# Gated recurrence and feed-forward kernel: y of blocks 0 and 1 from high and low parts, block 0 gated inside the second sweep, another order up to the second iteration

## The reference

```python
u = x @ W_in + b_in                       # 256 -> 64
g = sigmoid(x @ W_gate + b_gate)          # 256 -> 256
for t in range(4096):                     # the recurrence
    h = tanh(h @ A + u[t] @ Bm)
    y[t] = g[t] * (h @ C.T + u[t] @ D.T) + (1 - g[t]) * x[t]
x1 = layernorm(x + (y @ W_out + b_out + x))
hid = gelu(x1 @ bw1.T + b1)               # bw = mean|w| * sign(w), exact gelu
out = layernorm(x1 + (hid @ bw2.T + b2))
```

## Time and profile before

| | before |
|---|---|
| median of three | 446.37 us |
| profiled execution, its own time | 446.38 us |
| its span | 444.6 us |
| PE busy | 424.6 us, 96% |
| DVE busy | 361.0 us, 81% |
| ACT busy | 309.9 us, 70% |
| POOL busy | 302.3 us, 68% |

### The profile page before, as it was taken

How to read it: one execution, slowest core, us unless ns; L and a number is a source line. 1 busy time by engine, 2 the same in 40 slices (tenths; PEclk the granted TensorE clock), 3 DMA queues, 4 the chain that set the end, 5 groups by cost and what they waited for, 6 DMA issues and landing times.

```text
span 444.6 us, 8039 instructions
## 1 busy us (share of the span) xinstructions
PE 424.6 (96%) x2687; PEld 303.4 (68%) x2687; DVE 361.0 (81%) x791; ACT 309.9 (70%) x570; POOL 302.3 (68%) x302
## 2 busy tenths in 40 slices
PE   7999999999998899999999999999999999999882
PEld 4788887777554576776867767677676776766651
DVE  3666687744772889999999999999999999998584
ACT  1222224656446768798898988989889898797791
POOL 5199722242467697977979779797797977683523
PEclk9999999999999999999999999999999999999998
DMA  7944550000110112133331342313423134231222
GB/s 225 361 137 132 142 136 2 1 0 1 47 48 2 47 34 63 47 50 112 74 100 48 97 118 73 96 48 97 122 68 97 55 88 129 63 97 46 51 94 94
DMA packets 43893, 37.16 MB, mean 84 GB/s; under 512 B 35504, under 2 KB 37296, under 8 KB 43856
## 3 DMA queue, kind: packets, MB, share of 16 engines
q1 hardware_dynamic: 42528, 35.66, 28.7%
q0 software_dynamic: 272, 0.66, 0.6%
q10 hardware_dynamic: 1056, 0.36, 0.3%
HBM read 19.90 MB, written 8.39 MB: 64 GB/s over the span
## 4 chain that ended last, share of the span: by engine, by line
PE 59%; DVE 19%; POOL 8%; issue 5%; ACT 4%; DMA 4%; SPq 0%; DVEq 0%; POOLq 0%; ACTq 0%
PE bank L1016 15%; PE bank L1004 12%; PE bank L978 8%; PE bank L862 7%; DVE hid L1328 7%; PE bank L774 6%; PE bank L767 5%; DMA gT<-in_L_attn_x 4%; DVE bank L1311 3%; ACT hid L631 3%; DVE gT L1341 3%; PE bank L759 3%; PE bank L960 2%; DVE bank L1334 2%; DVE gT L1323 2%
## 5 line engine op out<-in xcount | busy, mean ns | idle before, releaser
L1004 PE MATMUL bank<-xT,w1s 128*128 128x512 f16 x512 | 127.1, 380 | 4.5 <-DVE hid L1328 3.8
L1016 PE MATMUL bank<-w2s,hid 128*128 128x256 f16 x1024 | 125.4, 273 | 1.1 <-DVE gT L1341 1.0
L1016 PEld LDWEIGHTS bank<-w2s,hid 128*128 128x128 f16 x1024 | 98.6, 98 | 31.6 <-issue 5.9
L623 ACT ACTIVATE bank<-bank,b_col,alpha 128x512 f32<-128x512 f32 x128 | 96.8, 756 | 18.8 <-PE bank L1004 18.4
L1328 DVE SCALAR_TENSOR_TENSOR hid<-bank,small,hid 128x512 f16<-128x512 f32 x128 | 94.4, 739 | 14.3 <-ACT hid L631 14.3
L631 ACT ACTIVATE hid<-bank,small 128x512 f16<-128x512 f32 x128 | 86.6, 692 | 19.0 <-PE bank L1016 17.8
L1004 PEld LDWEIGHTS bank<-xT,w1s 128*128 128x128 f16 x512 | 45.9, 98 | 51.1 <-DVE hid L1328 9.9
L407 POOL TENSOR_TENSOR ys_lo<-gT,ys_hi 128x512 fp32r<-128x512 f32 x32 | 40.8, 1277 | 26.3 <-ACT ys_hi L598 26.2
L403 POOL TENSOR_TENSOR gT<-gT,xT 128x512 f32<-128x512 f32 x32 | 40.8, 1276 | 24.4 <-DVE gT L1283 24.3
L774 PE MATMUL bank<-hu,w_rec 128*128 128x128 f32 x208 | 45.5, 300 | 1.0 <-DVE hu L1125 0.9
L423 POOL TENSOR_TENSOR gT<-x_rows,b_row 128x1024 f32<-128x1024 f32 x16 | 38.1, 2379 | 7.7 <-DMA xT<-gT 7.7
(11 more groups left out here) (135 smaller groups left out, 802.0 us busy)
## 6 DMA issues: line engine op xcount, KB each, us to landing
x_load<-in_L_attn_x SPq DMA_DIRECT2D x16, 512.0 KB, 3.5
gT<-in_L_attn_x SPq DMA_DIRECT2D x15, 512.0 KB, 3.7
out_rows<-gT SPq DMA_DIRECT2D x15, 512.0 KB, 2.6
gT<-in_L_ffn_w SPq DMA_DIRECT2D x2, 1024.0 KB, 12.1
gT<-in_L_attn_x SPq DMA_DIRECT2D x4, 128.0 KB, 2.9
out_rows<-gT SPq DMA_DIRECT2D x2, 256.0 KB, 2.0
xT<-gT SPq DMA_TRANSPOSE x28, 3.2
w_gate<-in_L_attn_W_gate ACTq DMA_DIRECT2D x1, 256.0 KB, 7.8
```

The source lines that it names most:

```text
L623: nc.scalar.activation(bank[which][:, :], bank[which][:, :], ACT.Gelu, bias=b1_col[:, c:c + 1], scale=alpha1[:, c:c + 1]).then_inc(s_gelu, 1)
L1004: done = nc.tensor.matmul(bank[which][:, :], w1s[:, c, k, :], x1T[:, n, :, part, :, k, :], start=(k == 0 and part == 0), stop=(k == KD - 1 ...
L1016: done = nc.tensor.matmul(bank[tile // 2][:, tile % 2 * DM:(tile % 2 + 1) * DM], hid[:, c % 3, part, tile * P:(tile + 1) * P], w2s[:, :, c ...
```

## The change

- `align`, the whole products of y and the copy `cd_t` are gone. y of blocks 0 and 1 is made of parts as for the others: in place of one product in full precision, three products of parts.
- Block 0 goes through it within the second sweep. DVE makes the high parts of `hu` (`first_y_high`), POOL the low ones, PE puts the three products for m = 0 and those for m = 1 behind the gate products of the first two steps of block 13 (`first_y`), and DVE does less x, times gate, plus x and the high part (`first_gated_y`). These live in parts of `gT` that are free then. `out_products(0, 0)` and `(0, 1)` follow right behind the sweep.
- If a guess was wrong, the repair redoes block 0.
- The order on PE, ACT, DVE and POOL is rewritten from the end of the sweep to iteration 1. The loop itself is unchanged.

```diff
+        y0_hu_hi, y0_hu_lo = (gT_parts[:, NB - 4, i].rearrange("p (s r) -> p s r", r=P) for i in range(2))
+        y0_hi = gT_parts[:, NB - 3]
+        y0_lo = gT_parts[:, NB - 2]
+        y0_stage = gT[:, NB - 1]
```

On POOL:

```diff
-            for n in range(0, GATED, 2):
-                pool.wait_ge(s_xgh[0], n // 2 + 1)
...
-            mix(0, 0)
-            mix(0, 1)
+            for n in (0, 2, 4, 6, 8):
+                gate_x_low(n)
+            hu_low(0, 0)
+            hu_low(0, 1)
+            gate_x_low(10)
             ys_low(0, 0)
             ys_low(0, 1)
...
             add_bias(0)
+            hu_low(1, 0)
             first_rstd(0, 0)
+
+            pool.wait_ge(s_rs1, 1)
+            hu_low(1, 1)
+            first_rstd(0, 1)
```

On ACT, behind the first gelus:

```diff
-            for c in range(4):
+            for c in range(3):
                 hidden_gelu(0, c)
                 hidden_hi(0, c)
-            hu_high(3, 0)
+            x1_hi(1, 0)
+            hidden_gelu(0, 3)
+            hidden_hi(0, 3)
+            x1_hi(1, 1)
```

On PE:

```diff
+            def first_y(s):
+
+                if s < KD:
+                    y_products(0, s)
...
-                gated_block(j, (j - B0 + 1) % 2, prepare_rows if j == PREP else None)
+                gated_block(j, (j - B0 + 1) % 2, prepare_rows if j == PREP else first_y if j == FIRST_Y else None)
...
             gate_half(GATED, 0, gate_parts, 1)
+            out_products(0, 0)
             pe.wait_ge(s_cmp, 3)
...
-            whole_y_products(0)
             gate_half(GATED, 1, gate_parts, 1)
-            gate_half(GATED + 1, 0, gate_product)
+            out_products(0, 1)
...
+            gate_half(GATED + 1, 0, gate_product)
             gate_half(GATED + 1, 1, gate_product)
+            y_products(1, 0)
+            y_products(1, 1)
             gate_half(GATED + 2, 0, gate_product)
-            pe.wait_ge(s_wsplit, 2)
-            for pair in range(2):
-                out_products(0, pair)
-            whole_y_products(1)
+            x1_transposes(0, 0)
             gate_half(GATED + 2, 1, gate_product)
+            x1_transposes(0, 1)
             gate_half(GATED + 3, 0, gate_product)
-            x1_transposes(0, 0)
             gate_half(GATED + 3, 1, gate_product)
+            out_products(1, 0)
+            out_products(1, 1)
             gate_half(GATED + 4, 0, gate_product)
-            x1_transposes(0, 1)
             gate_half(GATED + 4, 1, gate_product)
```

On DVE:

```diff
+            for half in range(2):
+                first_y_high(half)
+            gate_x_hi(9)
+            gate_x_lo(9)
+            less_x(0, 0)
+            first_gated_y(0)
+            gate_x_hi(10)
+            less_x(0, 1)
+            first_gated_y(1)
+            gate_x_hi(11)
+            gate_x_lo(11)
```

More of the change, by code:

```diff
@@ L82, in gated_rnn_ffn @@
         xT = sb("xT", [P, NB, KD, N])
+        with nc.sbuf_tensor("gT_parts", [P, NB, KD, N], F32R) as gT_parts:
+            pass
         gT = sb("gT", [P, NB, KD, N])
@@ L384, in _ @@
                 pool.tensor_tensor(sign, sign, negative, ALU.subtract).then_inc(s_sgn, 1)
[L387 to L391 removed]
             def hu_low(b, half):
[L394 to L395 removed]
+                pool.wait_ge(s_huhi, b * 2 + half + 1)
+                high, low = (hu_hi, hu_lo) if b > 0 else (y0_hu_hi, y0_hu_lo)
+                pool.tensor_tensor(low[HALVES[half], :, :], beside(b, half), high[HALVES[half], :, :].bitcast(F32),
                                    ALU.subtract).then_inc(s_hulo, 1)
[L398 removed]
+                pool.wait_ge(s_hulo, b * 2 + half + 1)
             def mix(b, m):
@@ L615, in hu_high @@
             def hu_high(b, half):
-                if half == 0 and b > WHOLE_Y:
+                if half == 0 and b > 1:
                     act.wait_ge(s_ymm, b * KD)
+                elif half == 0:
+                    act.wait_ge(s_gmm, (GATED + 1) * KD)
                 nc.scalar.activation(hu_hi[HALVES[half], :, :], beside(b, half), ACT.Copy).then_inc(s_huhi, 1)
@@ L719, in _ @@
             hidden_hi(0, 4)
+            hu_high(3, 0)
             hu_high(3, 1)
@@ L722, in _ @@
             hidden_hi(0, 5)
-            x1_hi(1, 0)
-            x1_hi(1, 1)
             for n in range(1, NB - 1):
@@ L1069, in _ @@
             pe.wait_ge(s_scale, 1)
-            out_products(1, 0)
+            y_products(2, 0)
             hidden(0, 0)
             hidden(0, 1)
-            y_products(2, 0)
             hidden(0, 2)
-            out_products(1, 1)
             y_products(2, 1)
+            ffn_out(0, 0)
             hidden(0, 3)
-            ffn_out(0, 0)
+            ffn_out(0, 1)
             hidden(0, 4)
-            ffn_out(0, 1)
+            x1_transposes(1, 0)
+            ffn_out(0, 2)
             hidden(0, 5)
-            ffn_out(0, 2)
+            x1_transposes(1, 1)
             ffn_out(0, 3)
             hidden(0, 6)
-            x1_transposes(1, 0)
             hidden(0, 7)
-            x1_transposes(1, 1)
             ffn_out(0, 4)
```

240 lines of the change are left out of this document (125 added, 115 removed).

## The result

The changed kernel takes 449.61 us, median of 10 runs (448.63 to 451.01), against 446.34 us for the kernel before (445.37 to 448.48, 10 runs) on the same chip: ratio 1.0072, 95% interval 1.0053 to 1.0092. The medians differ by 3.3 us; 449.1 us (445.9 to 450.8) was predicted. The profiled execution took 449.57 us, its span is 447.7 us (before 444.6). Four of the ten executions of the changed kernel took 450.43 to 451.01 us at a mean granted clock of 0.989 to 0.993, the other six, the profiled one among them, 448.63 to 449.64 us at 0.995 to 0.997.

What follows compares the result with a forecast made beforehand. PE was taken as the bound from the sweep to the loop, iteration 1's entry moving the end. Wait 2.4, matmuls 1.25, gate 11 0.5, work -2.03 and waits 0.6 gave +2.7 us: 449.1 us, range 445.9 to 450.8.

Steps and rivals of the forecast that it cites:

- The wait: Block 13 of the second sweep: PE waits 2.4 us for POOL's low parts of hu, DVE's cast getting in between.
- rival 2: Gate 9's cast goes first on DVE, making the wait in block 13 3.65 us; 450.3 us in all; chance 0.17.
- The moved matmuls: First two steps of block 13: two groups of y products, 1.40 us less 0.16 us to spare, add 1.25 us.
- Gate 11: DVE's cast and difference for gate 11 alternate with POOL's ys_low(0, .), costing PE about 0.5 us.
- Work behind the sweep: PE loses four whole products, -3.44 us, and gains y of block 1 in parts, +1.41: together -2.03 us.
- waits: Between sweep and iteration 1: old waits of 5.5 us vanish, new ones of 6.1 us come, +0.6 us.
- The single waits: New PE waits at y_products(1, 0), x1_transposes(0, 0), ffn_out(0, 0), ffn_out(0, 3), hidden(0, 7), y_products(3, .): 6.1 us in all.
- The sum: Whole kernel: wait 2.4, matmuls 1.25, gate 11 0.5, work -2.03, waits 0.6 make +2.7 us, 449.1 us.
- The marks: Trace signs: gate 11 at about 116.1 us, entry of iteration 1 at 162.7 us, then 18.42 us per iteration.
- 3: DVE and POOL don't block in this stretch: wait in block 13 1.35 us, none at gate 11; 448.1 us; chance 0.14.
- 4: The new order waits less: nine tenths of 6.1 us covered, 443.6 us, chance 0.08; part covered, 444.2 to 448, 0.14.
- rival 5: PE's clock falls in the wait in block 13, slowing the sweep's steps; 452 us or more; chance 0.05.

Runs made afterwards that it cites:

- e7: Changed kernel with first_y_high ahead of gate 7's cast on DVE and hu_low(0, .) right behind gate_x_low(6) on POOL; 446.77 us, ratio 1.0018 to the kernel before.
- e2: Changed kernel with DVE held before gate 9's cast until POOL has both low parts of hu of block 0; 449.71 us, ratio 1.0075 to the kernel before.
- e11: e2 again, the same kernel; 449.08 us, ratio 1.0073 to the kernel before.
- e6: e1 with the three products of parts of y(0, .) issued twice in block 13; 448.86 us, ratio 1.0073 to the kernel before.
- e3: Changed kernel with first_norm(0, 0) ahead of the four operations on y of block 1 on DVE; 447.85 us, ratio 1.0053 to the kernel before.
- e12: Changed kernel again, unaltered, as partner of e11 on one chip; 449.41 us, ratio 1.0080 to the kernel before.
- e1: Changed kernel with block 0's parts of hu ahead of gate 8's cast (DVE) and gate_x_low(8) (POOL); 447.44 us, ratio 1.0039 to the kernel before.
- e4: Changed kernel with the edits of e1 and e3 together; 446.32 us, ratio 1.0008 to the kernel before.
- e8: Changed kernel with e7's placing, e3's edit and orders rewritten from gate 12 to iteration 1; 441.05 us, ratio 0.9891 to the kernel before.

## Why the prediction was right

Its direction and its mechanism held, and the range. That the number came so close is in part luck, since its errors nearly cancelled. Step by step, what it said, and what was measured:

- *The wait, 2.4 us.* 2.0 us start to start in the profile, of which 1.89 us reach iteration 1 in e7. The mis-sized term of the sweep. POOL was first, at 100.76 us, as in the forecast (rival 2 needed it to come after DVE, which came at 101.01). I had POOL through with gate 8 at 100.7, 0.1 us after the first product of block 13; it was through 0.05 us before that product. And I let the cast of 0.69 us push POOL's pair back by nearly its whole length between the two operations, to 3.2 us. In fact the pair takes 2.95 us, 0.34 more than apart (e2: 2.61): the cast, which takes 0.9 us longer, pays most. The trace agrees with the rule of the Trainium skill (SBUF — State Buffer, Who interferes with whom): the cast and the difference of gate 9, and those of gate 11, grew by 0.9 us each beside POOL, and in e2 gate 9's, held apart from POOL, did not grow at all. What the blocking costs in all is another matter: undoing it at gate 9 gave nothing between the two points (e2, e11).
- *The moved matmuls, 1.25 us.* 3.4 - 2.0 = 1.4 us in the changed kernel, 1.3 in e7, and a second helping costs 1.44 us in e6.
- *Gate 11, 0.5 us.* From the last scan product (114.71) to gate 11 it is 1.27 us, before 0.94 (111.06 to 112.00): 0.33 us.
- *Work behind the sweep, -2.03, and waits, +0.6.* Together -1.43 was said and -0.87 measured. The recorded idle went from 4.25 to 5.00 us. By my estimate each wait is longer than recorded by the overlap of the product ahead, 0.39 - 0.23 = 0.16 us, and there are seven now against five before (PE's timeline of the kernel before shows 0.22, 0.69, 1.38, 1.83 and 0.17 us). So the new ones are 5.00 + 7 x 0.16 = 6.1 us, the forecast to the tenth, but the old ones 4.25 + 5 x 0.16 = 5.05, not 5.5: +1.05 us in place of +0.6. The work is not measured by itself; it is what is left, -0.87 - 1.05 = -1.9 us. So the mis-sized term here is the old waits, put 0.45 us too high.
- *The single waits.* Forecast 0.7, 1.5, 0.6, 0.75, 1.35, 1.0 and 0.2 us; recorded 0.57, 1.34, 0.29, 0.67, 1.18, 0.78 and 0.18 us, at the seven places named (with 0.16 us added to each, 0.73, 1.50, 0.45, 0.83, 1.34, 0.94 and 0.34). e3 confirms that x1 waits behind y of block 1 on DVE.
- *The sum, +2.7 us.* 3.4 + 0.33 - 0.87 = +2.9 us, and 0.23 us by which this profile's sweep began later. The medians say 3.3 us. The errors in the wait (-0.4), at gate 11 (-0.17), in the moved matmuls (+0.15) and behind the sweep (+0.56) nearly cancelled.
- *The marks.* Gate 11 at 116.1: 115.98. That is closer than it was right: counted from the first product of block 13, 15.57 us were forecast and 15.17 measured. Entry at 162.7: 163.15 (62.1 and 62.3 us from there). Stretch between them 46.6: 47.17. Period 18.42: 18.42 (the last window).
- *The rivals.* 2 and 3 fall by the rows above, 3 by the lengths of the casts. The row that the prediction had for operations that read PSUM (115.13 us) lies before POOL begins (116.71) and shows nothing of blocking; the one at 117.19 us, beside POOL, took 0.69 us too. 4 falls: none of the waits was covered. 5: in the profiled executions the clock stayed at 1.00 in a wait of 2.0 us, as the row on the program's end let expect. The Trainium skill's rule (TensorE: Matmul & The Clock Gate, HAM oscillation) speaks of longer gaps, and no run here tests it.
- *What rival 5 leaves open.* Of the other executions only the mean granted clock is known. It is 0.989 to 0.992 in 7 of the 25 executions of the three runs that keep the whole wait (changed, e3, e12), and never below 0.993 in the 58 executions of the nine other runs with the change, where the wait is shorter or gone. In the kernel before, which has no such wait, it is that low in 2 of the 56 beside e1 to e12. That speaks for a clock that falls in some executions with the wait, and against its being the only cause; where in the program it fell, no profile shows. These executions raise the medians: the other five of e3 have a median of 447.3 us in place of 447.85, which brings its saving nearer to the 1.5 us of the profile.

What the prediction did not see is that the order was worth more than the change. It counted the old waits, 5.5 us, only as something that disappears, and set 0.08 on the case that the new ones be covered. Both kernels hold some 5 us of waits between sweep and loop that a better order takes away, with the change (72.23 to 67.27 us from e4 to e8) or without (72.30 to 67.12).

## What to carry to other kernels

Work moved under a dependent chain is hidden only up to that chain's spare time per step; here, by estimate, 0.08 us against 0.70 us of products (1.3 of 1.4 us came out as time in e7), and a doubled dose costs its whole length. Before moving work to save time, sum the waits that the written order leaves in the same stretch and reorder the kernel as it is: it gave 1.2% where the change gave nothing. An operand made for a moved step needs its own place in the producers' queues; here an idle stretch of 6.3 us on POOL, one gate block ahead, took the parts without a wait of PE in the sweep.

## What the runs showed of the hardware

- DVE and POOL block each other unequally: DVE's cast begun beside a running pair of POOL operations takes 1.58 in place of 0.69 us, its difference of two SBUF operands 2.10 in place of 1.23, two casts of 64x512 1.84 us; POOL's pair only 2.95 in place of 2.61 us. Where more of DVE's work meets it, POOL loses more: its pair for `ys_low(0, .)` takes 3.17 in place of 2.49 us, that for `hu` in e7 3.17 in place of 2.60. Operations of DVE that read PSUM kept 0.69 us beside it (the one at 110.31 us in the changed kernel, beside `gate_x_low(10)`).
- A wait shortened by ordering two engines apart (0.34 us, twice) did not reach iteration 1 in the profiles, because the start of another DVE operation stayed where it was (21.27 and 21.24 us from the first product of block 13); what holds it is open.
- The same program's sweep reached block 13 at 101.59 us from the span's start in one profile (e2) and at 99.80 us in another (e11), with 2.4 and 0.4 us of recorded waits of PE for the first loads of x; the changed kernel at 100.81 and 99.86 us. Single profiles are to be compared from a common event on, not from zero.
